# Transposing the dequantized weight on TensorE while it is produced, instead of by DMA when it is first used

## What is computed

```
x = x + 0.5 * (LN(x) @ W.T + bias)         W = qweight * scales + scaled_zeros, 4096 x 4096
x = x + gelu(LN(x) @ A + b2)               A = (w1 @ w2.T) * sparse_mask,       4096 x 4096
x = x + 0.5 * (LN(x) @ W.T + bias)
```

## Time and profile before

| | us |
|---|---|
| median of 2 runs | 3508.61 (3492.31 to 3524.91) |
| the profiled execution | 3403.94 |
| its span on the slowest core (core 2) | 3402.4 |
| spans of the 8 cores | 3360.7 to 3402.4 |
| busy: TensorE, VectorE | 1935.1, 810.8 |

### The profile page before, as it was taken

The page is one execution under the profiler, slowest core; times in us unless marked ns, Lnnn a source line. Parts: engine busy times, 40 slices in busy tenths (PEclk is TensorE's granted clock), DMA queues, the critical chain, the costliest instruction groups (busy, mean ns, idle before and its releaser), DMA issues.

```text
span 3402.4 us, 25870 instructions; the slowest of 8 cores (3360.7 to 3402.4 us)
## 1 busy us (share of the span) xinstructions
PE 1935.1 (57%) x8280; PEld 843.6 (25%) x8280; DVE 810.8 (24%) x3395; ACT 168.7 (5%) x157; POOL 83.6 (2%) x144
## 2 busy tenths in 40 slices
PE   1344544730551544646664647498816996556986
PEld 0112221310220211213221222243303433222432
DVE  1234433140641351013000041400012002323000
ACT  0000000000000000021000021200020001120000
POOL 0000000000000000000000000000000000000000
PEclk9999999965875767867877857599957987666988
DMA  9789887699889789546565503135181350140443
GB/s 131 100 125 144 143 126 141 171 240 197 200 190 256 153 212 243 152 153 168 135 169 144 154 13 95 58 99 149 50 296 43 106 149 21 34 130 16 133 124 124
DMA packets 518288, 466.65 MB, mean 137 GB/s; under 512 B 275856, under 2 KB 478384, under 8 KB 503824
## 3 DMA queue, kind: packets, MB, share of 16 engines
q1 hardware_dynamic: 352976, 288.92, 29.2%
q0 software_dynamic: 28992, 108.98, 19.9%
q10 hardware_dynamic: 136192, 67.11, 8.0%
HBM read 407.47 MB, written 124.65 MB: 156 GB/s over the span
## 4 chain that ended last, share of the span: by engine, by line
PE 40%; DMA 16%; another core or an unknown queue 14%; DVE 12%; SPq 9%; issue 6%; ACT 2%; DVEq 1%; ACTq 0%; POOLq 0%
PE ps L530 27%; DMA w2bT<-w2t 9%; SPq L420 8%; PE pa L357 7%; DVE hT L596 3%; PE tr L510 3%; DVE w2t L282 2%; DVE x_sb L610 2%; DMA w2t<-w2bT 2%; PE ptr L342 2%; DVE wout L297 2%; DMA qt<-qw 2%; DVE h_tmp L585 2%; DMA x_sb<-x_in 1%
## 5 line engine op out<-in xcount | busy, mean ns | idle before, releaser
L530 PE MATMUL ps<-mv,hT 128*128 128x512 bf16 x4536 | 1084.9, 405 | 254.1 <-DMA mv<-wdq 129.2
L357 PE MATMUL pa<-w2t,w1blk 128*128 128x512 bf16 x1760 | 414.2, 400 | 474.5 <-DMA w1blk<-w 224.4
L530 PEld LDWEIGHTS ps<-mv,hT 128*128 128x128 bf16 x4536 | 464.2, 103 | 873.1 <-issue 406.1
L342 PE MATMUL ptr<-ident_bf,qt 128*128 128x128 bf16 x1024 | 226.4, 265 | 359.0 <-DVE w2t L282 247.9
L510 PE MATMUL tr<-ident_bf,h_tmp 128*128 128x128 bf16 x768 | 163.3, 266 | 355.6 <-DVE h_tmp L585 238.5
L357 PEld LDWEIGHTS pa<-w2t,w1blk 128*128 128x128 bf16 x1760 | 178.8, 102 | 709.6 <-issue 524.4
L610 DVE SCALAR_TENSOR_TENSOR x_sb<-ps,x_sb 128x512 f32<-128x512 f32 x128 | 80.8, 687 | 1107.9 <-PE ps L540 1107.9
L282 DVE COPY w2t<-ptr 128x128 bf16<-128x128 bf16 x1024 | 200.7, 222 | 383.6 <-PE ptr L342 235.7
L297 DVE TENSOR_SCALAR wout<-qt,scl_sb,zro_sb 128x128 bf16<-128x128 bf16 x1024 | 231.2, 311 | 96.8 <-DMA qt<-qw 96.8
L342 PEld LDWEIGHTS ptr<-ident_bf,qt 128*128 128x128 bf16 x1024 | 106.6, 104 | 478.6 <-issue 464.3
L510 PEld LDWEIGHTS tr<-ident_bf,h_tmp 128*128 128x128 bf16 x768 | 80.0, 104 | 440.7 <-issue 431.4
(11 more groups left out here) (31 smaller groups left out, 134.2 us busy)
## 6 DMA issues: line engine op xcount, KB each, us to landing
mv<-wdqT SPq DMA_DIRECT2D x24, 4096.0 KB, 17.7
w2t<-w2bT SPq DMA_DIRECT2D x14, 4096.0 KB, 38.0
w1blk<-w POOLq DMA_DIRECT2D x16, 2048.0 KB, 45.1
qt<-w POOLq DMA_DIRECT2D x32, 1024.0 KB, 13.3
w2bT<-w2t ACTq DMA_DIRECT2D x32, 1024.0 KB, 17.6
qt<-qw POOLq DMA_DIRECT2D x32, 1024.0 KB, 16.6
wdq<-wout ACTq DMA_DIRECT2D x32, 1024.0 KB, 13.6
wdqT<-mv SPq DMA_DIRECT2D x8, 4096.0 KB, 14.2
```

The costliest lines, as they stand in the source:

```text
L342: t.transpose(ptr[b % 2][:], qt[:, (r % 2) * D + blk * 128: (r % 2) * D + blk * 128 + 128], ident_bf[:]).then_inc(w2tr, 1)
L357: ins = t.matmul(pa[k % 2][:], w1blk[:, dc * 1024 + st * 128: dc * 1024 + st * 128 + 128], w2t[:, (qq % 2) * NC * 512 + dc * 512: (qq % 2) ...
L530: t.matmul(psb[j][:], hT[:, ic * 512 + j * 128: ic * 512 + j * 128 + 128], mv[:, sl + ii * 512:sl + ii * 512 + 512], start=(ii == 0), stop ...
```

## The change

1. The transposed W is now assembled in phase 1. TensorE, after tile k for k = 8 to 39, transposes the 32 blocks of dequantized row tile r = k-8 from `wout`. VectorE, after the multiplication of tile k, copies them to a new buffer `asm2` (two halves), and only then dequantizes tile k-6. ACTq stores the row tile straight to `wdqT`, in runs of 128 elements (256 bytes). The tensor `wdq` is gone.
2. In phase 2, p = 0 of u = 0 loads from `wdqT` with one instruction per group, as the other steps do. The 256 DMA transposes and the 8 stores of 4 MB are gone.
3. There are four PSUM buffers `ptr` in place of two, for both kinds of transposes: transpose b waits for the copy of block b-4.
4. The mask has two buffers in place of three: mask k waits for the multiplication of tile k-2.

```diff
-                mkt = es_1.enter_context(nc.sbuf_tensor("mkt", [128, 3 * 512], F32))
+                mkt = es_1.enter_context(nc.sbuf_tensor("mkt", [128, 2 * 512], F32))
+                asm2 = es_1.enter_context(nc.sbuf_tensor("asm2", [128, 2 * D], BF16))
...
                 ptr = [es_1.enter_context(nc.psum_tensor(f"ptr{i}", [128, 128], BF16))
-                       for i in range(2)]
+                       for i in range(4)]
...
                         for k in PAIR_TILES[qq]:
                             Sg = K_TILES[k][3]
-                            if k >= 3:
-                                sync.wait_ge(p1_ev, k - 2)
+                            if k >= 2:
+                                sync.wait_ge(p1_ev, k - 1)
...
                     def dequant_tile(r):
                         v.wait_ge(q_ld[r % 2], 16 * (r // 2 + 1))
                         if r >= 2:
-                            v.wait_ge(q_st[r % 2], 16 * (r // 2))
+                            v.wait_ge(wqtr, 32 * (r - 1))
...
                         ).then_inc(p1_ev, 1)
+                        if 8 <= k < 40:
+                            r = k - 8
+                            if r >= 2:
+                                v.wait_ge(q_st[r % 2], 16 * (r // 2))
+                            for blk in range(NC):
+                                b = r * NC + blk
+                                v.wait_ge(wqtr, b + 1)
+                                v.tensor_copy(
+                                    asm2[:, (r % 2) * D + blk * 128:
+                                         (r % 2) * D + blk * 128 + 128],
+                                    ptr[b % 4][:],
+                                ).then_inc(wqev, 1)
                         if 6 <= k < 38:
                             dequant_tile(k - 6)
...
                     for r in range(32):
-                        s.wait_ge(q_dq, 32 * (r + 1))
-                        s.dma_start(out=wdq[r * 128:(r + 1) * 128, :],
-                                    in_=wout[:, (r % 2) * D:(r % 2) * D + D]
+                        s.wait_ge(wqev, 32 * (r + 1))
+                        s.dma_start(out=wdqT.rearrange("(c p) o -> p c o", p=128)
+                                    [:, :, r * 128:(r + 1) * 128],
+                                    in_=asm2[:, (r % 2) * D:(r % 2) * D + D]
+                                    .rearrange("p (c o) -> p c o", o=128)
                                     ).then_inc(q_st[r % 2], 16)
...
+                    def wq_transpose_tile(r):
+                        t.wait_ge(q_dq, 32 * (r + 1))
+                        for blk in range(NC):
+                            b = r * NC + blk
+                            if b >= 4:
+                                t.wait_ge(wqev, b - 3)
+                            t.transpose(ptr[b % 4][:],
+                                        wout[:, (r % 2) * D + blk * 128:
+                                             (r % 2) * D + blk * 128 + 128],
+                                        ident_bf[:]).then_inc(wqtr, 1)
...
                             ins.then_inc(p1_pe, 1)
+                            if 8 <= k < 40:
+                                wq_transpose_tile(k - 8)
...
-                                elif u == 0 and p == 0:
-                                    sync.wait_ge(q_st[0], 16 * (2 * oc + 2))
-                                    sync.wait_ge(q_st[1], 16 * (2 * oc + 2))
-                                    for ic in range(NC):
-                                        sync.dma_start(
...
                                 else:
+                                    if (u, p, oc) == (0, 0, 0):
+                                        sync.wait_ge(q_st[0], 256)
+                                        sync.wait_ge(q_st[1], 256)
                                     sync.dma_start(
```

More of the change, by code:

```diff
@@ L96, in mv_slot_done @@
 def mv_slot_done(u, p, oc):
-    tot = [0, 0]
-    for uu in range(2):
-        for pp in range(3):
-            for oo in range(8):
-                g = (uu * 3 + pp) * 8 + oo
-                tot[g % 2] += 512 if (uu, pp) == (0, 0) else 16
-                if (uu, pp, oo) == (u, p, oc):
-                    return tot[g % 2]
-    raise AssertionError
+    g = (u * 3 + p) * 8 + oc
+    return 16 * (g // 2 + 1)
 def build_nc():
@@ L152, in build_nc @@
     w2ev = sem1("w2ev")
+    wqtr = sem1("wqtr")
+    wqev = sem1("wqev")
     q_ld = semn("q_ld", 2)
@@ L156, in build_nc @@
     wt_ld = semn("wt_ld", 2)
-    mk_ld = semn("mk_ld", 3)
+    mk_ld = semn("mk_ld", 2)
     p1_st = semn("p1_st", 2)
@@ L284, in _ @@
                                     (r % 2) * D + blk * 128 + 128],
-                                ptr[b % 2][:],
+                                ptr[b % 4][:],
                             ).then_inc(w2ev, 1)
@@ L305, in _ @@
                         v.wait_ge(p1_pe, k + 1)
-                        v.wait_ge(mk_ld[k % 3], 16 * (k // 3 + 1))
+                        v.wait_ge(mk_ld[k % 2], 16 * (k // 2 + 1))
                         if k >= 2:
@@ L339, in _ @@
                             b = r * NC + blk
-                            if b >= 2:
-                                t.wait_ge(w2ev, b - 1)
-                            t.transpose(ptr[b % 2][:],
+                            if b >= 4:
+                                t.wait_ge(w2ev, b - 3)
+                            t.transpose(ptr[b % 4][:],
                                         qt[:, (r % 2) * D + blk * 128:
@@ L404, in _ @@
                                 if p == 1:
-                                    if u == 0 and oc <= 1:
-                                        sync.wait_ge(te_st, 128)
                                     S0, nk = ATT_SC[oc][0], len(ATT_SC[oc])
```

25 lines of the change are left out of this document (4 added, 21 removed).

## The result

| | before | changed kernel |
|---|---|---|
| median of the timed runs, us | 3475.4 (26 runs) | 3483.6 (27 runs) |
| ratio | | 1.0087, 95% interval 1.0047 to 1.0127 |
| profiled execution, span of the slowest core | 3402.4 | 3464.0 |
| spans of the cores, median | 3383 | 3439 |

The changed kernel is 0.9% slower, and the whole interval lies above 1. The forecast was 1.7% faster. Against 3475, the ratio is 30 us.

What follows compares the result with a forecast made beforehand. Three stages were slow, held by stores and copy round trips, late `w2t`/`w1` loads, and DMA transposes on SyncE's queue. -112 - 60 + 115 = -57 us: 3404 becomes 3347, by medians 3450; own range 3390 to 3525, whole 3370 to 3560.

Steps and rivals of the forecast that it cites:

- Part 1, phase 2: First use of W: without DMA transposes the step falls from 381 to 271 us, 2 more behind it; -112 us.
- Part 2, first stage: Transposing w2 in phase 1: four `ptr` buffers cut a row's copies to 6.0 us; -60 us, bounds -30 and -95.
- the steady turn comes to rest nearer 26.6: First stage: DMA work of 26.6 us per two rows, not 23.6, limits the turn; -3.1 us for 11 turns.
- Part 3, the longer turns: Second stage of phase 1: VectorE's multiplication, copies and dequantization make a turn 14.0 us.
- Part 4, two mask buffers: Second stage: each next `w2t` load is released one multiplication later; with the longer turns, stage sum +115 us.
- one turn later: Second stage: `w2t` load released by the last tile but two, not but three; landing then taken as 60 us.
- The increments of the stretches 13 to 20, 20 to 26, 27 to 35 and 35 to 41: Second stage: turns of 14.0 us to the releasing tile, then the landing; +18, +18, +24, +24 us.
- The terms for the two `w1` stretches, +11 and +6: Second stage, tiles 11, 12 and 26: POOL issues the `w1` load later, after dequantization behind the copies; +11 and +6 us.
- The second rival: 256-byte stores land late and hold VectorE's copies; second stage +200, first stage gives nothing, +88 in all, 3492 us; chance 0.11.
- Its condition (22 us): Second stage: a store must land within 22 us, before the copies two turns on; beyond that the stores decide.
- the first rival: Second stage: beside small pieces `w2t` loads land sooner, in 38.0 us; stage +23, -149 in all, 3255 us; chance 0.28.

Runs made afterwards that it cites:

- a_w2run8: Changed kernel with `w2bT` stored and loaded in 8 KB runs, matmuls of the second stage reading their columns as four pieces; ratio 0.9396 to the kernel before.
- b_ptr4: Kernel before with four `ptr` buffers in place of two, nothing else; ratio 0.9891 to the kernel before.
- a_ptr2: Changed kernel with two `ptr` buffers again in place of four, for both kinds of transposes; ratio 1.0291 to the kernel before.
- b_mk2: Kernel before with two mask buffers in place of three, nothing else; ratio 1.0091 to the kernel before.
- a_wqrun8: Changed kernel with W stored as it lies in `asm2` and loaded in 8 KB runs, phase 2 matmuls reading four pieces; ratio 0.9867 to the kernel before.
- b_w2run8: Kernel before, with its two `ptr` buffers, and `w2bT` in 8 KB runs; ratio 0.9441 to the kernel before.
- a_all: Changed kernel with `w2t` loads issued early and both transposed weights in 8 KB runs; ratio 0.9308 to the kernel before.

## Why the prediction was wrong

- **Part 1, phase 2: right.** -112 forecast. From the first matmul to the last adding the step took 272 us on the median core (379 before), where 271 was forecast. 5 us are given back ahead of it. The whole of phase 2 became 107 us shorter.
- **Part 2, first stage: mechanism wrong.** The step "the steady turn comes to rest nearer 26.6" failed: it rested at 29.5. I had taken the share of busy time of the DMA engines, 0.81, for room that faster copies could fill. a_w2run8 shows that the short runs of the stores were the bound: the same engines moved the same bytes in 337 us where the changed kernel took 493. In the profiles the stage ended 13 us sooner (forecast 60, bounds 30 to 95). The 38 us by the times of b_ptr4 lie within the bounds by luck: most of them came from the slowest core, which no term of the sum had.
- **Part 3, the longer turns: right in size at first.** 14.2 us where 14.0 were forecast, later in the stage up to 16.5, since a tile's matmuls took 8 to 10 us and not 7.2 between the transposes. a_ptr2 shows that the stage follows the turn in part.
- **Part 4, two mask buffers: the step "one turn later" failed.** It costs 24 us (b_mk2), 15 of them in the tiles 0 to 6 (forecast 7). In between the landing shortens by about what the issue is late. The increments of the stretches 13 to 20, 20 to 26, 27 to 35 and 35 to 41 were forecast as 18, 18, 24, 24 and came out as 20, 19, 23, 25, but for another reason: with 8 KB stores they were 11, 15, 19 and 26 (a_wqrun8), which is the longer turns for the most part, and the rest came with the 256-byte stores. That they agree so well is luck.
- **The terms for the two `w1` stretches, +11 and +6, were the mis-sized ones.** They measured +31 and +20. The sum had the longer turns in them, but not the store: one in 256-byte runs that is in flight beside a `w1` load takes as long as the load (87 us), and holds VectorE, and through its dequantization POOL, which issues the `w1` load. On the median core the first of these loads was issued 54 us after the first matmul of tile 11 (27 before, 38 forecast) and the second 36 us after that of tile 26 (18 before, 24 forecast), and they landed in 83 and 80 us (79 and 76 before). With 8 KB stores they were issued after 40 and 24 us and landed in 71 and 70, and the stretches were at +5 and -2 (a_wqrun8).

The second stage came to +172 instead of +115, over the 170 from which the prediction itself called its sum failed: 34 more in the `w1` stretches, 13 more in the tiles 0 to 6, and some 9 behind tile 41. In the profiles the parts are -13, +172 and -107, which makes +52 where the median spans differ by 56. The times moved less, +30. In part this is because the profiled execution of before was a quick one (median span 3383, where that of the others is 3395), in part because the slowest core stood some 55 us above the median core before the change and 31 after it. With 8 KB stores the second stage is at +112, which is nearly the forecast; but its terms are others, so this is luck too. The measured median of 3483.6 us lies inside the stated ranges (3390 to 3525, and 3370 to 3560 as a whole) although the sign was wrong: they were wide, and they started from 3508.6, the median of two runs, where 26 runs gave 3475.

The second rival, that the 256-byte stores are the bound, was the nearest to what happened. Its condition (22 us) was met only while a `w2t` or `w1` load was in flight, and its price came true in part: it had put the second stage 85 us above the forecast, and 57 were measured. In the first stage it held for the steady turn, which did not shorten. The rule of the Trainium skill beside the first rival ("DMA: Bandwidth & Descriptors", "Queues, rings and completion order") would have had the loads beside small pieces land sooner. The `w2t` loads for the tiles 20, 26 and 35 did land in 50, 53 and 47 us (median core) where 66, 68 and 68 stood, as the rule has it. But b_mk2, with 8 KB stores and the later issue, had 56, 58 and 56, and a_wqrun8, which has the turns of the changed kernel and 8 KB stores, 49, 55 and 54. So the later issue accounts for most of it and leaves at most some 7 us for the rule. In a_w2run8, where loads in 8 KB runs stand beside 256-byte stores of W, they took 36, 32 and 38 us, in b_w2run8 beside 8 KB stores 51, 56 and 53. That goes the rule's way, but the turns of these two differ as well, so it stays open. What neither the rule nor I had weighed is the other side, the small pieces' own landing.

What stays open: how much of the remaining 90 us in the second stage of the changed kernel (over b_mk2, with the stores mended) is VectorE's work and how much TensorE's slower tiles. The transposes were not tried without their copies.

## What to carry to other kernels

A DMA share below 1 is not room: in this kernel transfers in short runs bounded a stage at 0.85, and what was made faster beside them was given back as a longer landing. Before moving work onto an engine, look at how the data leaves it. Storing a transposed tile as it lies in SBUF, and letting the matmul read its columns in four pieces, was worth 5.6% in one kernel (b_w2run8) and 6.9% in the other (a_w2run8 against the changed kernel), while the change as it stands made the kernel 0.9% slower. And where a wait is removed and the total stays, look for the wait that had lain beside it: here late loads, 256-byte stores and queued masks covered one another, and the early loads, worth nothing alone, gave 27 us beside 8 KB stores of W.

## What the runs showed of the hardware that had not been expected

- 256-byte stores stretch with what flies beside them: 7.0 us for the shortest, 23 beside the loads of w2, and 24 to 87 for 13 of the 32 stores of W, each with a `w2t` or `w1` load in flight (changed kernel). Stores of the same megabyte in 8 KB runs took 4.7 to 15.6 us beside the loads of w2 (a_w2run8) and 3.9 to 13.6 in the second stage (a_wqrun8).
- TensorE reading its moving operand in four pieces of 128 columns cost nothing visible: the first step of phase 2 took 271.7 us in the changed kernel and 271.2 in a_wqrun8, from first matmul to last adding (median core).
- A small load behind a 4 MB load in one queue lands with it: mask and `w2t` load landed within 1 us of each other in four of the five cases of a_all.
- Between transposes, 32 matmuls of 512 columns took 8 to 10 us (670.76 to 1263 us of the changed kernel), where six tiles in a row took 7.4 each (tiles 0 to 5, 44.24 us). The granted clock over the stage was 0.73, before the change 0.74, so the mean clock does not tell the two kernels apart.
